# A mixture-of-experts router with a fixed area of 1024 rows for each expert, scattered in two halves

## What is computed

```python
x = x + 0.5 * ffn_ternary(norm(x))        # 256 -> 1024 -> 256, weights -1, 0, 1
x = x + attention(norm(x))                # 16 heads of 16, causal, rope
x = x + 0.5 * ffn_ternary(norm(x))
x = x + 0.5 * experts(norm(x))            # first expert stage, u = 0
x = x + mamba(norm(x))                    # 512 channels, 16 states
x = x + 0.5 * experts(norm(x))            # second expert stage, u = 1

def experts(x):                           # 16 experts of 256 -> 128 -> 256
    shared = swiglu(x, wg_s, wu_s, wd_s) * 0.1       # 256 -> 256 -> 256
    affinity = sigmoid(x @ centroids.T)              # 1024 x 16
    _, top = top_k(affinity + gate_bias, 2)
    w = take(affinity, top); w = w / (w.sum(-1) + 1e-9)
    return shared + sum_j w[:, j] * swiglu_of_expert(top[:, j], x)
```

## Time and profile before

| | |
|---|---|
| runs (us) | 893.64, 893.75, 898.28; median 893.75 |
| profiled execution (us) | 904.27, of which the profile's span is 903.0 |
| PE busy | 740.1 us, 82% |
| DVE busy | 592.3 us, 66% |
| ACT busy | 371.9 us, 41% |
| POOL busy | 352.0 us, 39% |
| DMA | 65.98 MB, 73 GB/s over the span |
| mean granted TensorE clock | 0.917 |
| first expert stage | about 341 to 453 us of the span |
| second expert stage | about 785 us to the end |

### The profile page before, as it was taken

How to read it: one execution, slowest core, us unless ns; L and a number is a source line. 1 busy time by engine, 2 the same in 40 slices (tenths; PEclk the granted TensorE clock), 3 DMA queues, 4 the chain that set the end, 5 groups by cost and what they waited for, 6 DMA issues and landing times. The chain is left out here.

```text
span 903.0 us, 11468 instructions
## 1 busy us (share of the span) xinstructions
PE 740.1 (82%) x3883; PEld 484.0 (54%) x3883; DVE 592.3 (66%) x1010; ACT 371.9 (41%) x752; POOL 352.0 (39%) x426
## 2 busy tenths in 40 slices
PE   3978899889898897699579787979778888788990
PEld 2766454344433674578446454545445554455880
DVE  6977635766541787345277977788997798772333
ACT  3321324345566242023227744687544545221330
POOL 3124223102221301626510355657566667234462
PEclk9998668698999999899889989999799999899996
DMA  4945722020000921256220000000060000013435
GB/s 179 300 62 84 101 37 38 2 37 2 1 1 1 372 92 36 101 176 201 86 91 0 1 1 0 2 1 0 1 244 36 1 0 1 36 36 130 132 121 180
DMA packets 37497, 65.98 MB, mean 73 GB/s; under 512 B 11474, under 2 KB 27474, under 8 KB 35810
## 3 DMA queue, kind: packets, MB, share of 16 engines
q1 hardware_dynamic: 32930, 52.87, 20.8%
q0 software_dynamic: 4512, 12.39, 3.8%
HBM read 39.63 MB, written 21.69 MB: 68 GB/s over the span
## 5 line engine op out<-in xcount | busy, mean ns | idle before, releaser
L1306 PE MATMUL PS<-FB,C 128*128 128x512 f32 x256 | 137.7, 635 | 3.8 <-DVE FB L1975 3.5
L1411 ACT ACTIVATE FA<-PS 128x512 f32<-128x512 f32 (+3 forms) x192 | 80.6, 499 | 67.2 <-PE PS L1054 66.9
L2052 POOL TENSOR_SCALAR_AFFINE_SELECT FA<-FA 128x128 f32<-128x128 f32 x128 | 36.2, 293 | 126.4 <-ACT FA L1411 124.1
L2111 POOL TENSOR_TENSOR FB<-FB,RBF 128x512 f32<-128x512 f32 x51 | 65.8, 1291 | 49.2 <-DVE FB L1966 48.9
L2087 POOL DMA_INDIRECT GY<-FB x62 | 61.6, 993 | 53.5 <-issue 26.7
L1697 DVE TENSOR_REDUCE FA<-PS 128x2 f32<-128x1024 f32 (+2 forms) x64 | 67.8, 1085 | 17.2 <-PE PS L1033 17.0
L916 PE MATMUL PS<-TRI 128*128 128x512 bf16 x233 | 60.3, 402 | 16.2 <-DMA FB<-GY 12.1
L1054 PE MATMUL PS<-RA 64*128 64x512 f32 (+3 forms) x192 | 59.0, 482 | 5.1 <-ACT FA L1411 4.9
L1187 PE MATMUL PS<-WE,FB 128*128 x248 | 59.1, 380 | 0.7 <-ACT FB L1443 0.7
L1306 PEld LDWEIGHTS PS<-FB,C 128*128 128x128 f32 x256 | 46.5, 201 | 21.4 <-issue 11.6
L1054 PEld LDWEIGHTS PS<-RA 64*128 64x128 f32 x192 | 28.5, 213 | 51.4 <-ACT FA L1411 30.3
(11 more groups left out here) (274 smaller groups left out, 1642.4 us busy)
## 6 DMA issues: line engine op xcount, KB each, us to landing
WE<-in_wr SPq DMA_DIRECT2D x8, 1536.0 KB, 10.7
FB<-GX SPq DMA_DIRECT2D x14, 520.0 KB
RA<-RA SPq DMA_DIRECT2D x48, 128.0 KB, 4.8
FB<-GY SPq DMA_DIRECT2D x8, 512.0 KB, 5.7
GX<-GX SPq DMA_DIRECT2D x1, 4030.0 KB, 25.5
GX<-FA SPq DMA_DIRECT2D x1, 3968.0 KB, 16.5
FA<-in_w SPq DMA_DIRECT2D x2, 1024.0 KB, 7.1
FA<-in_qkvo SPq DMA_DIRECT2D x1, 1536.0 KB, 20.1
```

Of the source, the lines that this page charges most:

```text
L1306: pe.matmul(bank(m), ident, shc[k % 4], start=n == 0, stop=n == DN - 1).then_inc(*yad.inc(ch, n, m))
L1411: act.activation(PT[n % 12][:, c0:], bank(ring_bank[(x, *a)])[:, c0:], ACT.Exp, scale=0.25).then_inc(*exd.inc(*a))
L2111: pool.tensor_tensor(shc[k % 4], sh[k % 5], Cs[(stc.no[ch, n] - 1) % 2], ALU.mult).then_inc(*cma.inc(ch, n, m))
```

## The change

`GX` becomes one area of 16 x 1024 rows, used by both stages: expert e owns rows 1024 e and on, so a row's target is 1024 times its expert plus its place among the expert's rows, and needs no base. That splits the routing by chunk:

- `top` and `rank` of chunk 0 stand before the normalisation of chunk 1; `rank` is one matmul for the places within the tile row and one for each earlier tile, and `pos` three DVE operations for a chunk. Chunk 0's eight scatters (two copies of four tiles) are issued before chunk 1 is routed. Their indices are `i12`.
- The second copies have their own rows, `XT2`, in the two `xin` buffers: ACT copies the 256 columns, POOL writes both sets of ids.
- The blocks are worked out later (`count`, `blocks`): the expert of each of 31 blocks, and its first row in `GX`, `rowno`. SP fetches block by block: a register load (`value_load`) and one DMA of 128 rows each, instead of one DMA for four.
- The ids of padding rows are no longer in `GX`. `filled` works out for every row of a block whether it is past the expert's rows, and `ids` (now on DVE, two operations) puts a spare id there; the step stands behind `e4` and `back`.
- All of `GX` is zeroed once, in four DMAs of 4096 rows: one at the start, three in the attention, behind the placement of the maxima of heads 1, 2 and 3 of chunk 1. The spare ids' DMA and the copy to `GX[1]` go.
- The shared expert's order is (n, ch) = (0,0), (1,0), (0,1), (1,1), with other banks (`SB`); gate and up are separate steps, and the gate of (0,0) stands between the scores and the turn of chunk 1. The first pair waits for its fetch only, behind 16 fillers; the second pair waits for the shared add.
- Fillers: 3 instead of 5 and 7 ahead of the turns of chunk 1, 6 and 2 ahead of the two ranks.

```diff
     yield [("mld", u)]
-    yield [("route", u, 0)]
+    yield [("route", u, 0), ("rows", u, 0)]
     stat0, stat1, rstd, nrm0, nrm1, tr, xn0, xn1 = norm_steps(s, 1)
-    yield stat0 + stat1 + rstd + nrm0 + nrm1
-    yield [("rows", u), ("top", u, 0)] + tr + xn0 + xn1
-    yield [("route", u, 1), ("top", u, 1), ("rank", u), ("wsp", u)]
-    yield [("sgu", u, 0, 0), ("pos", u), ("scat", u), ("wts", u)]
-    yield [("sgu", u, 0, 1), ("smid", u, 0, 0), ("sgu", u, 1, 0), ("smid", u, 0, 1), ("sdn", u, 0, 0)]
-    yield [("sgu", u, 1, 1), ("smid", u, 1, 0), ("sdn", u, 0, 1), ("smid", u, 1, 1), ("sdn", u, 1, 0), ("sdn", u, 1, 1)]
-    yield [("sadd", u), ("fetch", u, 0), ("fetch", u, 1)]
+    yield stat0 + stat1 + rstd + [("top", u, 0), ("rank", u, 0)] + nrm0 + nrm1
+    yield [("rows", u, 1), ("pos", u, 0), ("scat", u, 0)] + tr + xn0 + xn1 + [("wsp", u)]
+    yield [("route", u, 1), ("sgu", u, 0, 0, "g"), ("top", u, 1), ("sgu", u, 0, 0, "u"), ("rank", u, 1), ("smid", u, 0, 0)]
+    yield [("pos", u, 1), ("scat", u, 1), ("count", u), ("blocks", u)]
+    def gate_up(n, ch):
+        return [("sgu", u, n, ch, "g"), ("sgu", u, n, ch, "u")]
+    yield gate_up(1, 0) + [("smid", u, 1, 0)] + gate_up(0, 1) + [("smid", u, 0, 1)] + gate_up(1, 1) + [("sdn", u, 0, 0)]
+    yield [("smid", u, 1, 1), ("sdn", u, 1, 0), ("sdn", u, 0, 1), ("sdn", u, 1, 1)]
+    yield [("sadd", u), ("fetch", u, 0), ("fetch", u, 1), ("filled", u), ("wts", u)]
     aside = iter([[x] for k in range(len(MW)) for x in (("mwl", k), ("mws", k))]) if u == 0 else iter(())
...
             b = PAIRS[i][1]
             gi = (b - 1) // WB
-            if i % 2 == 0:
-                yield [("ids", u, gi)]
             if (b % WB == 0 or b == NB) and gi + 2 < len(GROUPS):
                 yield [("fetch", u, gi + 2)]
         if 0 <= i - 1 < n:
...
             yield [("e4", u, i - 3), ("back", u, i - 3)]
+        if i < n and i % 2 == 0:
+            yield [("ids", u, (PAIRS[i][1] - 1) // WB)]
...
-                    sp.dma_start(gx3[0][:, :, 0:D], zt.unsqueeze(1).broadcast_to([P, NB, D])).then_inc(*gz.inc(0, "zero"))
+                    sp.dma_start(GX[0:4 * S, :].rearrange("(b p) d -> p b d", p=P), zt.unsqueeze(1).broadcast_to([P, 4 * NT, RW])).then_inc(*gz.inc(0))
...
-                    sp.dma_start(gx3[0][:, :, D:RW], cst("spare").rearrange("p (b n) -> p b n", b=NB)).then_inc(*gz.inc(0, "spare"))
...
+                    if ch and g:
+                        e0, e1 = NZ[g]
+                        sp.dma_start(GX[e0 * S:e1 * S, :].rearrange("(b p) d -> p b d", p=P), zt.unsqueeze(1).broadcast_to([P, 4 * NT, RW])).then_inc(*gz.inc(g))
                 elif x == "late":
-                    sp.wait_ge(*gz.at(0, "spare"))
-                    sp.dma_start(GX[1], GX[0]).then_inc(*gz.inc(1, "copy"))
...
-                        sp.wait_ge(*scat[0].at(u, 1, NT - 1))
-                        sp.wait_ge(*scat[1].at(u, 0, NT - 1))
+                        sp.wait_ge(*scat.at(u, 1, 1, TC - 1))
+                        sp.wait_ge(*eidd.at(u))
-                    sp.dma_start(xin[gi % 2].rearrange("p (b n) -> p b n", n=RW)[:, 0:b1 - b0, :], gx3[u][:, b0:b1, :]).then_inc(*fet[gi % 2].inc(u, gi))
+                    for b in range(b0, b1):
+                        v = sp.value_load(rowno[0:1, b:b + 1], min_val=0, max_val=NE * S - P)
+                        sp.dma_start(xin[gi % 2][:, (b - b0) * RW:(b - b0) * RW + RW], GX[bass.ds(v, P), :]).then_inc(*fet[gi % 2].inc(u, b))
...
                 elif x == "rank":
+                    u, ch = a
+                    to = bank(ch)[:, 64:128]
+                    if u and ch == 0:
+                        pe.wait_ge(*mlx.at(TC - 1))
+                    busy(bank(5), 2 if ch else 6)
+                    pe.wait_ge(*hotd.at(u, ch))
+                    pe.matmul(to, TRI[:, 0:P], mb[:, ch * TC:ch * TC + TC, :], start=True, stop=False, skip_group_check=True)
+                    for v in range(ch * TC + 3):
+                        j = max(0, v + 1 - ch * TC)
+                        t = pe.matmul(to[:, 16 * j:64], TRI[:, P:2 * P], mb[:, v, :].unsqueeze(1).broadcast_to([P, TC - j, 16]),
+                                      start=False, stop=v == ch * TC + 2, skip_group_check=True)
+                    t.then_inc(*rkd.inc(u, ch))
+                    if ch:
+                        group(bank(4)[:, 0:16], [(TRI[:, P:2 * P], mb[:, v, :]) for v in range(NT)]).then_inc(*rkd.inc(u, "all"))
                 elif x == "sgu":
+                    u, n, ch, part = a
+                    at = 0 if part == "g" else P
+                    if (n, ch) == (0, 1):
+                        pe.wait_ge(*posd.at(u, part == "u"))
+                    elif part == "g":
+                            pe.wait_ge(*wsl.at(u, n))
+                        else:
+                            pe.wait_ge(*smd.at(u, 0, 0))
+                    to = bank(SB[n, ch] + (part == "u"))
+                    group(to, [q for k in range(2) for q in three([v[:, k * 256 + at:k * 256 + at + P] for v in WS[n]], xn(k, ch))]).then_inc(*sgu.inc(u, n, ch, part))
                 elif x == "sdn":
+                    if (n, ch) == (0, 0):
+                        pe.wait_ge(*eidd.at(u))
+                    hh = HS[(2 * ch + n) % 3]
...
                     if pi == 0:
-                        busy(bk, 26)
+                        busy(bk, 16)
+                    elif pi == 1:
                     if pi % 2 == 0:
-                        pe.wait_ge(*fet[gi % 2].at(u, gi))
+                        pe.wait_ge(*fet[gi % 2].at(u, GROUPS[gi][1] - 1))
                     if pi > 1:
...
+                elif x == "rows":
+                    u, ch = a
+                    act.wait_ge(*nrm.at(3 + 2 * u, ch, 1))
+                    if u and ch == 0:
+                        act.wait_ge(*gtl.at(1, 3))
+                    act.activation(XT2[ch][:, :, 0:D], XTs[:, ch * TC:ch * TC + TC, 0:D], ACT.Copy).then_inc(*x2c.inc(u, ch))
+                elif x == "sgu" and a[3] == "g":
+                    u, n, ch, _ = a
...
                 elif x == "rank":
+                    u, ch = a
+                    T = slice(ch * TC, ch * TC + TC)
+                    dve.wait_ge(*d_own.at())
+                    dve.tensor_tensor(o12[:, T], cst("iota")[:, 0:16].unsqueeze(1).unsqueeze(1).broadcast_to([P, TC, 2, 16]),
+                                      ix[:, T, 0:2].unsqueeze(3).broadcast_to([P, TC, 2, 16]), ALU.is_equal).then_inc(*d_own.inc())
+                    dve.wait_ge(*d_own.at())
+                    dve.tensor_tensor(mb[:, T, :], o12[:, T, 0, :], o12[:, T, 1, :], ALU.add).then_inc(*hotd.inc(u, ch))
                 elif x == "pos":
+                    u, ch = a
+                    T = slice(ch * TC, ch * TC + TC)
+                    c4 = cb128[:, 0:32 * TC].rearrange("p (t j e) -> p t j e", t=TC, j=2)
+                    r = bank(ch)[:, 64:128].rearrange("p (t e) -> p t e", t=TC)
+                    dve.wait_ge(*rkd.at(u, ch))
+                    dve.tensor_tensor(c4, o12[:, T], r.unsqueeze(2).broadcast_to([P, TC, 2, 16]), ALU.mult).then_inc(*d_own.inc())
+                    dve.wait_ge(*d_own.at())
+                    dve.reduce_sum(s12[:, T, :], c4, AX).then_inc(*d_own.inc())
+                    dve.wait_ge(*d_own.at())
+                    dve.scalar_tensor_tensor(i12[:, T, :], ix[:, T, 0:2], float(S), s12[:, T, :], ALU.mult, ALU.add).then_inc(*posd.inc(u, ch))
+                elif x == "count":
+                    dve.wait_ge(*rkd.at(u, "all"))
+                    dve.memset(one16, 1.0)
+                    dve.memset(step, 0.0)
+                    dve.tensor_copy(cnt, bank(4)[:, 0:16])
+                    dve.tensor_scalar(nblk.bitcast(U32), bank(4)[:, 0:16], float(P - 1), None, ALU.add).then_inc(*d_own.inc())
+                elif x == "blocks":
+                    u, = a
+                    past = cb128.rearrange("p (b e) -> p b e", e=16)
+                    iota = cst("iota")
+                    dve.tensor_scalar(step[:, 0:NE - 1], base[:, 0:NE - 1], -float(P), float(S), ALU.mult, ALU.add)
+                    dve.tensor_tensor(base, endb, base, ALU.subtract)
+                    dve.tensor_tensor(past, iota[:, 0:NB].unsqueeze(2).broadcast_to([P, NB, 16]), endb.unsqueeze(1).broadcast_to([P, NB, 16]), ALU.is_ge).then_inc(*d_own.inc())
+                    dve.wait_ge(*d_own.at())
+                    dve.scalar_tensor_tensor(upto, base, float(P), cnt, ALU.mult, ALU.add)
+                    dve.reduce_sum(es, past, AX).then_inc(*d_own.inc())
+                    dve.wait_ge(*d_own.at())
+                    dve.tensor_tensor(past[0:1], past[0:1], step[0:1, :].unsqueeze(1).broadcast_to([1, NB, 16]), ALU.mult)
+                    dve.tensor_scalar(es, es, float(NE - 1), None, ALU.min).then_inc(*d_own.inc())
+                    dve.wait_ge(*d_own.at())
+                    dve.tensor_scalar(eid[0:1, :], es[0:1, :], 768.0, None, ALU.mult)
```

(41 more changed lines are left out.)

155 lines of the change are left out of this document (38 added, 117 removed).

## The result

The changed kernel took 889.23 us (median of 20 runs), the kernel before 899.25 in the 20 runs beside them: a ratio of 0.9887, 95% interval 0.9862 to 0.9911. That is 1.1% faster; 1.9% was forecast. On the 893.75 us of the three runs shown before, the ratio gives 883.7, inside the range of 867 to 888; the median itself is 1.2 us above it. The three runs shown were low for this kernel: twenty have a median 5.5 us higher.

The account below looks back on a forecast made before the run. A chain of waits bounds the kernel: the second stage waits for scatters, the first for PE's order. Stages save 8.4 and 9.6, together 18; 17 off the 893.75 us median gives 876.8 us, range 867 to 888.

Parts of the forecast that it names:

- First scatter: Routing: the first scatter starts once chunk 0 has its indices, at 792.3 in the second stage, 349.7 in the first.
- The train of 16: POOL's 16 scatters of a stage: without two copies and waits between (0.9 us) they take 19.6 us.
- Last scatter to turn: SP's fetches before PE's first turn: 1.1 us a block, the turn 6.2 us after SP is free.
- Rows against PE: Before the first turn: PE is ready 1.4 us before the fetched rows in both stages.
- Behind the turn: After the first turn: late second group costs 1.2 us a stage, late mamba weights 1.4 in the first stage.
- Clearing: Zeroing GX: three writes in the attention are covered by 24.5 us or more between placements; cost 0.
- Rival D: Attention: clearings take longer than 24.5 us and hold placements; at 35 us, 895, no change; chance 0.03.
- rival C: Scatters beside a busy DVE: ten scatters 0.7 us longer each, a stage loses 7, 890; chance 0.08.
- rival B: Block loop: SP's fetches pace it above 1.62 us a block; at 2.0, 905, slower; chance 0.07.
- SP's register load: SP's load of a block's first row: 0.30 us, as PE's load took, within 1.1 us a block.
- rival E: Both stages: no late second group, no late weights, the median with the full idle: 871; chance 0.14.
- rival A: Shared expert: PE idles again for its last product, first turn 3 us late in each stage, 883; chance 0.20.

Follow-up runs that it names:

- late: The changed kernel, but chunk 0's eight scatters wait until chunk 1's places are written too; 1.0062 of the kernel before, on chip 10.
- before_b: The kernel before the change, profiled once more without an edit, on chip 6; ratio 1.0015, stages 106.6 and 105.6 us.
- pad: The changed kernel with 20 filler matmuls between the shared expert's up and down parts; 0.9845 of the kernel before, on chip 6.
- regs_b: The changed kernel with SP loading a group's four block addresses ahead of its wait, run on chip 12; 0.9814 of the kernel before.
- clearlate: The changed kernel with the last three clearings of GX moved behind the expert weights' load; 0.9922 of the kernel before, on chip 6.
- regs: The changed kernel with SP loading a group's four block addresses ahead of its wait, run on chip 10; 0.9946 of the kernel before.
- again_b: The changed kernel itself, run once more without an edit, on chip 12; 0.9878 of the kernel before.
- combo: The changed kernel with early address loads, each block pair waiting for its own fetches, first mamba weights between the first two groups; 0.9774 of before, chip 12.
- pair: The changed kernel with every pair of blocks waiting for its own two fetches alone; 0.9872 of the kernel before, on chip 6.

## Why the prediction was right or wrong

The mechanism was right: 16 scatters set the rows, the rows set the turn, and starting them 10 us earlier pays (late). The direction and the sign of every term came out. The size did not: 11.7 between the two profiles shown, 11.8 to 13.1 between before_b and the changed kernel's three others, 10.0 in the medians, against 18 and 17. The step that failed is the start and length of the scatters, put 2.9 us too early and 1.1 us too short in the two stages together; the cover of rows over PE failed beside it. Term by term, with the times of the profile after moved by the difference of the two additions (11.92 us in the second stage, 3.73 in the first):

- **First scatter.** 792.3 forecast, 792.9 measured. The indices were there at 792.1; POOL then waited for ACT's copy of the chunk (1.06), which the forecast counted for chunk 1 and not for chunk 0. First stage 349.7 forecast, 352.0; 1.7 of that is this execution's own (its clock was 0.66 over the chunk's scoring; fourteen other profiles have 9.5 us from the addition instead of 11.2), the rest the copy again.
- **The train of 16.** 19.6 forecast, 20.5 and 19.8. I had taken 0.9 of copies and waits out of before's 20.5. POOL in before, around the first copy:

```profile
813.06 0.98 POOL L2065 DMA_INDIRECT GX<-FB  x1 [0.30 <-issue]
...
814.53 0.98 POOL L2072 DMA_INDIRECT GX<-FB  x1 [0.28 <-issue]
```

Between these two scatters lie 0.49 us, and 0.55 around the second copy, where 0.30 stands between any two. So only 0.44 could be taken out; and four scatters of the second stage took 1.1 to 1.6, one more than before. Over all profiles of the new order the train is 19.8 to 20.5.
- **Last scatter to turn.** 8.7 forecast, 9.2 (9.6 in two others). A block costs SP 1.10, as forecast from PE's load of 0.30. But the first address is loaded behind the wait: SP issues at +3.50 instead of +2.5, and only part of it came back in the fetches.
- **Rows against PE.** PE was to be ready 1.4 ahead of them. It was 4.63 and 3.79 ahead, since PE was 1.2 early and the rows 2.0 late in the second stage. I called it a thin cover and weighed only that PE might be late; in the first stage PE was 0.5 late and the rows 2.7. What the idle time does to the clock stood nowhere in the forecast: a term put at nothing without a reason.
- **Behind the turn.** 1.2 and 2.6 us lost were forecast; it is 1.9 and 3.0 against the profile shown. The second group's wait is there once the clock is up (0.85 and 0.90 in pad and regs_b). Against before_b, which has the same low clock, next to nothing is lost behind the turn (0.4 more in the first stage, 0.5 less in the second): the forecast's base happened to be a profile with the clock up.
- **Clearing.** 0 forecast, none found: 14.5 to 15.8 us each, under the cover of 24.5. Rival D is out (clearlate).
- **Scatters beside a busy DVE** (rival C): spacing 1.27 in DVE's busiest stretch (4.69 of 5 us) as in its idlest. Out. The rule of the Trainium skill ("SBUF — State Buffer", section "SBUF: two separate sides") is that a two-port DVE operation locks GpSimd out of writing descriptors. The trace shows no such loss; which of DVE's operations in that stretch are of that kind, no row tells.
- **SP as the bound** (rival B): 1.10 us against the 1.62 from which it begins. Out.
- **SP's register load.** 0.30 forecast, 0.27 measured (median of 62). By the Trainium skill, "DMA: Bandwidth & Descriptors", section "Latency and other measured facts", the floor is about 600 ns; the trace disagrees, on SP as on PE.
- **More saved** (rival E): out, the second group and the weights were late.
- **PE decides** (rival A): not in the profile shown, nor on chips 6, 9 and 12. On chips 10 and 7 it is what happens wherever PE has work beside the last scatters, at a price of 12 to 13 us and not the 6 that I gave it. The 6.49 of the earlier trace rows that spoke for it was the slow stretch. It hits the new order harder than the old one: medians of before are 900 to 901 on chips 6, 9 and 12 and 903 to 905 on 10 and 7, while regs lost 12 more than before did by the ratios (8 by the medians, 886.0 and 896.6). Why it should: the scatters now start 10 us earlier, and the late reports, from 7 to 9 us behind the first of them, fall on the whole shared expert. That is argued from rows, not shown by a run of before against after on such a chip.

Second stage: -8.4 forecast; 0.6 for the first scatter, 0.9 for the train, 0.5 for the fetch and 0.7 behind the turn make -5.7, as measured. First stage: -9.6; 2.3, 0.2, 0.1, and 1.0 behind the turn make -6.0. The step that carries most of the miss is thus the first in the chain, the start and length of the scatters (4.0 of the 6.3 us; 1.7 of it chance, and in again_b, without that chance, still 2.9 of 4.7). The rest is the fetch (0.6) and what lies behind the turn (1.7). That the sum of before's stages was right is luck: the profile had PE held up and the clock up, before_b neither, and 212.4 and 212.2 come out of both. The raw median also missed for a plainer reason: I anchored it on three runs that were 5.5 us low.

## What to carry to other kernels

When a wait ends in a queue that first computes an address, load the address ahead of the wait: four lines gave 5 us of the two stages here, where nothing else was late. When a train of indirect DMAs is moved, look at what the other engines do beside its new place, and profile on more than one chip before believing the gain. Filler matmuls pay only if they end where the data lands: combo lost 3 us with 2 fillers in place of 16, and the changed kernel nothing.

## What the runs showed of the hardware

On two of five chips, from 7 to 9 us behind the first of 16 indirect scatters, what PE had finished reached ACT and DVE up to 12 to 13 us late (in regs, a product done at 354.35 was taken up at 366.76), and from 15.6 us on PE issued one instruction in 0.71 us until the last had landed. It costs 12 to 13 us of this kernel. Under the scatters at the end of the first stage the same showed in small (2.8 us in the run late). What causes it was not found: it may be a matter of the chip, of the count of scatters or of PE's rate of instructions, and no kernel here varied these on such a chip. An indirect scatter of 128 rows of 1040 bytes holds POOL 0.96 us, with 0.30 between two, whatever DVE does; three or four in sixteen took 1.1 to 1.6. PE's clock fell to its lower level when PE had idled 2.23 us or more for the first rows, or 1.83 and 2.04 with four turns between (pair); it stayed up after 1.2 and 1.3 (regs_b, combo).
